# A fused four-layer decoder on one core: the masked attention's bias half on VectorE, the row maxima's split on GpSimd, and a new step table

## What is computed

```python
scores = jnp.einsum('bhqd,bhkd->bhqk', Q, K) / jnp.sqrt(jnp.float32(D))
scores = scores + adj[None, None, :, :]
scores = jnp.where(mask == 0, jnp.float32(-jnp.inf), scores)
weights = jax.nn.softmax(scores, axis=-1)
out = jnp.einsum('bhqk,bhkd->bhqd', weights, V)
```

## Time and profile before

| | us |
|---|---|
| median of 3 runs | 1161.64 (1161.58 to 1163.73) |
| the profiled execution | 1165.91 |
| its span | 1164.2 |
| PE busy / DVE busy / ACT busy / POOL busy | 1086.9 / 907.9 / 690.8 / 330.2 |

### The profile page before, as it was taken

One profiled execution on the slowest core, in us unless ns is written; L12 is line 12 of the kernel. 1 busy time (PEld: TensorE's weight loads), 2 busy tenths in 40 slices (PEclk: granted clock), 3 DMA queues, 4 the chain that ended last, 5 costly groups with the idle time before them and its releaser, 6 DMA issues. The chain is left out here.

```text
span 1164.2 us, 24274 instructions
## 1 busy us (share of the span) xinstructions
PE 1086.9 (93%) x8050; PEld 691.2 (59%) x8059; DVE 907.9 (78%) x2316; ACT 690.8 (59%) x1488; POOL 330.2 (28%) x443
## 2 busy tenths in 40 slices
PE   6877989999999998999999999999899999999998
PEld 2223554567777775677544444665667676775576
DVE  6999788977898898666679972417899999987754
ACT  4544687865545559775656544446566566558562
POOL 4546222112121111012213323211474445421010
PEclk9989698999999999999989999999999999999999
DMA  8003243222312331134423433141010001114211
GB/s 251 1 0 101 79 145 124 67 74 92 93 58 82 104 107 56 39 101 124 133 83 105 165 147 119 33 134 32 15 51 1 1 19 42 60 34 155 66 42 60
DMA packets 75785, 93.00 MB, mean 80 GB/s; under 512 B 6536, under 2 KB 60272, under 8 KB 73840
## 3 DMA queue, kind: packets, MB, share of 16 engines
q1 hardware_dynamic: 74640, 89.34, 24.5%
q0 software_dynamic: 1024, 2.10, 0.6%
HBM read 64.25 MB, written 28.67 MB: 80 GB/s over the span
## 5 line engine op out<-in xcount | busy, mean ns | idle before, releaser
L1449 ACT ACTIVATE P<-bank 128x512 f32<-128x512 f32 (+1 forms) x448 | 228.5, 585 | 68.3 <-PE bank L1142 67.3
L1864 DVE TENSOR_REDUCE mx<-bank 128x2 f32<-128x512 f32 x320 | 200.2, 684 | 23.7 <-PE bank L1113 20.9
L1662 POOL TENSOR_SCALAR rstd<-mv 128x2 f32<-128x2 f32 x56 | 14.0, 250 | 452.1 <-DVE mv L1714 376.5
L1157 PE MATMUL bank<-P,V 128*32 128x256 f32 (+1 forms) x1536 | 101.7, 383 | 1.1 <-ACT P L1449 0.8
L1256 PE MATMUL bank<-xT,room 128*128 128x256 f32 x384 | 95.4, 386 | 0.0
L1262 PE MATMUL bank<-room 128*128 128x256 f32 x384 | 94.8, 385 | 0.0
L1113 PE MATMUL bank<-QKR 48*128 48x256 bf16 (+1 forms) x896 | 82.1, 278 | 8.9 <-ACT P L1449 3.9
L1142 PE MATMUL bank<-QKR 50*128 50x256 bf16 (+1 forms) x896 | 84.5, 277 | 3.4 <-ACT P L1449 1.3
L1672 POOL TENSOR_TENSOR qk<-qk,parts 128x256 f32<-128x256 f32 x56 | 38.3, 705 | 145.9 <-ACT parts L1418 145.9
L1256 PEld LDWEIGHTS bank<-xT,room 128*128 128x128 f32 x384 | 69.6, 190 | 16.5 <-issue 7.9
L1262 PEld LDWEIGHTS bank<-room 128*128 128x128 f32 x384 | 69.8, 190 | 14.7 <-issue 6.8
(11 more groups left out here) (288 smaller groups left out, 2381.2 us busy)
## 6 DMA issues: line engine op xcount, KB each, us to landing
QKR<-split_rows SPq DMA_DIRECT2D x112, 192.0 KB
room<-gate_rows SPq DMA_DIRECT2D x48, 256.0 KB, 3.7
split_rows<-parts SPq DMA_DIRECT2D x56, 192.0 KB, 2.3
split_rows<-parts SPq DMA_DIRECT2D x56, 128.0 KB, 2.0
room<-in_w SPq DMA_DIRECT2D x6, 1024.0 KB
room<-in_w SPq DMA_DIRECT2D x3, 2048.0 KB
split_rows<-parts SPq DMA_DIRECT2D x56, 64.0 KB, 1.7
room<-in_mask SPq DMA_DIRECT2D x4, 512.0 KB, 6.0
```

The source lines that it names most:

```text
L1157: last = nc.tensor.matmul(bk[32 * j:32 * j + 32, q0:S], V[:, n % 2, t, 8 * half + 4 * r + j, :], P[:, (e - 1 + j) % NBUF_P, t * S:t * S + ...
L1449: nc.scalar.activation(P[:, (e - 1) % NBUF_P, 0:width], psum(st, p)[:, 0:width], ACT.Exp, scale=SCALE).then_inc(read[k], 1)
L1864: V_.reduce_max(to, sc[:, :].rearrange("p (t s) -> p t s", t=TPB), AX.X).then_inc(read[k], 1)
```

## The change

1. `BY_PE` is 1: PE adds the bias through identity products to the first head of a pair only. For the second one DVE adds `biasf[:, 1]` to the scores in PSUM, writes the sum to `P`, and ACT exponentiates it there in place. The bank is given free by ACT's instruction, as before.
2. MS is done by POOL: a cast of `mx` to bfloat16 and a subtraction, positive, where DVE had negated; the rows of ones in `QKR` become -1.0. DVE waits, before the first maxima of a unit, until the splits of two units earlier are done.
3. Semaphores: `first_max` counts maxima for POOL, `biased` DVE's additions; `select_in` and `dz_exp` are folded into others.
4. `ORDER` is another string, for changed costs of these steps (P2 of MASKED 1.65 to 0.96 on PE plus 0.7 on DVE, MS 0.6 on POOL, STAT 1.1 instead of 0.95 on POOL). 2392 steps, FILL 130 matmuls instead of 129.

```diff
-BY_PE = 2
+BY_PE = 1
-    "BIAS": ((DVE, 1.15),), "SM": ((PE, 0.28), (DVE, 1.2)), "MS": ((DVE, 0.36),), ...
+    "BIAS": ((DVE, 1.15),), "SM": ((PE, 0.28), (DVE, 1.2)), "MS": ((POOL, 0.6),), ...
     if st[0] == "P2" and st[1] == MASKED:
-        return ((PE, 1.65), (ACT, 1.0))
+        return ((PE, 0.96), (DVE, 0.7), (ACT, 1.0))
 ORDER = (
-    "aaaaaaaababaccbebddacebaecbdaecdacbeddacebaebcdaceddbbaecacebbddaecaceddbabecacdedbbaecbdaecdacedbaceedbacebacdedbbaaecc"
+    "aaaaaaaababaccbebdacebddaecbaecdacebdabcebdaecbdacebdacedaceddbacedbabecbacebdaecbdacebdaecbddaeceaceddbabaeccdebndonabc"
...
@@ scalar engine, P2
+                        if st[1] == MASKED and p >= BY_PE:
+                            act.wait_ge(biased, NPAIR * st[2] + st[3] + 1)
+                            nc.scalar.activation(P[:, (e - 1) % NBUF_P, :], P[:, (e - 1) % NBUF_P, :], ACT.Exp, scale=SCALE).then_inc(read[k], 1)
+                            continue
@@ gpsimd
-            nc.gpsimd.memset(QKR[:, :, 1], 1.0).then_inc(consts, 1)
+            nc.gpsimd.memset(QKR[:, :, 1], -1.0).then_inc(consts, 1)
+                elif k == "MS":
+                    _, a, b, h = st
+                    n = unit[(a, b)]
+                    finished(pool, ("SM", a, b, HALF * h + HALF - 1))
+                    if a in (CAUSAL, MASKED):
+                        pool.wait_ge(first_max, causal_before(("SM", a, b, HALF * h + HALF - 1), 1))
+                    if n >= 2:
+                        full(pool, ("MT", units[n - 2][1], units[n - 2][2], h))
...
+                    link(nc.gpsimd.tensor_copy(hi, top_of))
+                    nc.gpsimd.tensor_tensor(low, top_of, hi, ALU.subtract).then_inc(shift_done, 1)
@@ vector, SM
+                    if i == 0 and unit[(a, b)] >= 2:
+                        dve.wait_ge(shift_done, 2 * unit[(a, b)] - 2)
@@ vector
-                elif k == "MS":
...
-                    link(V_.tensor_scalar(hi, top_of, -1.0, None, ALU.mult))
-                    V_.scalar_tensor_tensor(out=low, in0=top_of, scalar=-1.0, in1=hi, op0=ALU.mult, op1=ALU.subtract).then_inc(shift_done, 1)
+                elif k == "P2" and st[1] == MASKED:
+                    e = head_no(st, 1)
+                    if e > NBUF_P:
+                        full(dve, weighs(e - 1 - NBUF_P))
+                    dve.wait_ge(filled[k], e)
+                    V_.tensor_tensor(P[:, (e - 1) % NBUF_P, :], psum(st, 1)[:, :], biasf[:, 1, :], ALU.add).then_inc(biased, 1)
@@ vector, BIAS
+                        dve.wait_ge(biased, NPAIR * b)
```

More of the change, by code:

```diff
@@ L61 @@
     "MY": ((DVE, 0.9), (PE, 0.4)),
-    "STAT": ((DVE, 1.2), (POOL, 0.95)), "XB": ((POOL, 0.8),), "STAT2": ((DVE, 1.95), (POOL, 0.95)), "NORM": ((DVE, 0.62),), "XT": ((PE, 0.22), (ACT, 0.33)),
+    "STAT": ((DVE, 1.2), (POOL, 1.1)), "XB": ((POOL, 0.8),), "STAT2": ((DVE, 1.95), (POOL, 1.1)), "NORM": ((DVE, 0.62),), "XT": ((PE, 0.22), (ACT, 0.33)),
     "GQ": ((PE, 0.43), (ACT, 0.3)), "GS": ((PE, 0.43), (DVE, 1.7)), "GT": ((PE, 0.44), (ACT, 0.5)), "GM": ((PE, 0.86), (ACT, 0.3)),
@@ L65 @@
     "V": ((PE, 0.44), (DVE, 0.42)), "Z": ((PE, 0.86), (ACT, 0.48)),
-    "BIAS": ((DVE, 1.15),), "SM": ((PE, 0.28), (DVE, 1.2)), "MS": ((DVE, 0.36),), "MT": ((PE, 0.2), (ACT, 0.3)), "SHIFT": ((SP, 1.4),),
+    "BIAS": ((DVE, 1.15),), "SM": ((PE, 0.28), (DVE, 1.2)), "MS": ((POOL, 0.6),), "MT": ((PE, 0.2), (ACT, 0.3)), "SHIFT": ((SP, 1.4),),
     "P2": ((PE, 0.27), (ACT, 0.95)), "PA": ((PE, 0.95),), "PV": ((PE, 0.95), (ACT, 0.33)), "ZV": ((PE, 0.95), (DVE, 0.86)),
@@ L99, in cost @@
     if st[0] == "P2" and st[1] == MASKED:
-        return ((PE, 1.65), (ACT, 1.0))
+        return ((PE, 0.96), (DVE, 0.7), (ACT, 1.0))
     if st[0] == "STAT":
-        return ((DVE, 2.7 if SUBLAYERS[st[1]] == ("moe", DISPATCHED) else 1.55 if st[1] in RMS_SUBLAYERS else 1.2), (POOL, 0.95))
+        return ((DVE, 2.7 if SUBLAYERS[st[1]] == ("moe", DISPATCHED) else 1.55 if st[1] in RMS_SUBLAYERS else 1.2), (POOL, 1.1))
     if st[0] == "SM" and st[1] == MASKED:
@@ L481 @@
[L481 to L484, removed]
@@ L835, in full, with causal_before @@
             eng.wait_ge(filled[st[0]], banks_of(st) * count[st])
+        split_maxima = [st for st in steps if st[0] == "SM" and st[1] in (CAUSAL, MASKED)]
+        def causal_before(st, p):
+            return 2 * split_maxima.index(st) + p + 1
         def head_no(st, p):
@@ L983, in _ @@
                     full(sp, ("DO", 1, NBLOCK - 1))
-                    load(select, "select", select_in)
-                    load(one_of, "one_of", select_in)
+                    load(select, "select", lin_loaded)
+                    load(one_of, "one_of", lin_loaded)
                 elif st[:2] == ("LD", "ctx"):
```

66 lines of the change are left out of this document (31 added, 35 removed).

## The result

The change makes the kernel slower. In twelve runs each, the changed kernel takes 1169.91 us in the median (1165.80 to 1175.19) and the kernel before 1163.14 (1159.96 to 1169.47): ratio 1.0058, 95% interval 1.0038 to 1.0077. Measured once more later, beside other kernels, it was 1167.62 against 1162.97, ratio 1.0050 (1.0025 to 1.0075). The forecast was 1158, faster.

A forecast was written before the change was run, and what follows sets the result against it. PE was taken as the bound, with DVE only 9.7 us behind in the masked stage's first part. Terms -2.2 (masked stage) and -1.5 (early stages) gave -3.7 us: 1161.6 to 1157.9, said as 1158; range 1149 to 1169.

The forecast's parts named there:

- The start of the masked stage: Part 4's first step: moved steps make MASKED's first maxima start 3.3 us earlier, at 605.2 instead of 608.5.
- the early relief: From 120 to 600 us, DVE sheds most of 40 splits; PE idles less, gaining 1.5 us (0 to 5).
- DVE's work up to the last maxima: Masked stage: DVE's work rises from 73.2 to 90.4 us, a stretch of 97.4 us with its idle time.
- the last maxima themselves: Masked stage: last maxima done at 702.6 us, against 691.3 before; the early relief not yet taken off.
- The splits off the path: Part 3: splits on POOL come 0.1 to 0.6 us later plus a hop, covered by other PE work, costed at nothing.
- the rival by DVE's queue: Masked stage: additions waiting for P2 hold up maxima; over 11 us of DVE idle, 1166 us; chance 0.22.
- PE's tail in part 4: Masked stage, last score product to last P2: 8.1 us of P2 steps plus 9.9 other work, ending 2.2 us earlier.
- slower, by POOL's queue: Rival: SPLITs queue behind splits of maxima, late rows stall PE; one stall and clock fall 5.2 us, time 1165; chance 0.11.
- a few us of DVE at most and hardly on the path: Part 3: POOL's 28 us of new work holding up DVE instructions through shared SBUF interfaces.
- The sign of being wrong that was met: PE waiting for the rows' DMA more often than three times.
- part 5: Outside the masked stage: 1.5 us gained from 120 to 600 us; after MASKED's last P2, PE work unchanged within 1 us.
- part 4's reasoning: Masked stage to its last P2: DVE becomes the bound, so 22.6 us less PE work buys only 2.2 us.

The follow-up runs named there:

- t4_msonly: Kernel before, old step table, with only the splits of the maxima moved from DVE to POOL: 1166.74 us, ratio 1.0008 to the kernel before.
- r_after: The changed kernel itself, run and profiled a second time: 1167.62 us in the median, ratio 1.0050 to the kernel before.
- t12_allfills: The change with its last 621 steps in the old order and idle products ahead of masked-stage waits and other lulls: 1155.37 us, ratio 0.9945 to the kernel before.
- t1_newtable: Kernel before with only the new step table and costs, products still on PE and splits on DVE: 1197.40 us, ratio 1.0266.
- t5_dummy3: The change with three identity products per masked P2 put back on PE, their result overwritten: 1184.45 us, ratio 1.0160 to the changed kernel.
- t9_morefills: The change with idle products ahead of masked-stage waits and 37 more at its other lulls, new tail kept: 1166.63 us, ratio 1.0025 to the kernel before.

## Why the prediction was wrong

**What held.** The start of the masked stage: first maxima at 602.5 where 603.7 had been forecast with the early relief (605.2 less 1.5). How much of it the moved steps did was not tried by itself: the kernel before had falls at 460 and 588 us, of 3.4 us each, that the change doesn't have, and the change has others. Up to there the kernel before was granted 1.6 us less of the full clock than the change. DVE's work up to the last maxima, 91.3 against 90.4, and the last maxima themselves, 701.6 against 701.1. The additions, 0.692 against 0.688 us, and DVE above 90% there (92%), PE below 85% (83%); the stretch of 99.0 us lies between the 95 and 100 that had been named. POOL's 31.5 us more against 28. The splits off the path (t4_msonly). DVE did not idle for 11 us; it was 7.7, so the rival by DVE's queue is not what happened.

**The step that failed first is PE's tail in part 4,** the term of 18.0 us in "697.8 + 18.0 = 715.8". PE's last score product ended at 696.2, as forecast with the early relief (697.8 less 1.5). From there to the end of the last P2 it took 22.9 us, not 18.0, and 23.1 in r_after: from 692 to 708 us the clock was between 0.50 and 0.76. In t12_allfills, at the full clock, it took 20.2, with nine idle products in it. In r_after the stretch ahead of the tail was shorter by as much as the tail was long, so its last P2 came when it had been forecast; that is luck. I had put such a fall under "slower, by POOL's queue", once, for 5.2 us, with a chance of 0.11. It came four times in the stage, and three times in r_after. I had written down the two facts that make it likely, a dozen us of new idle time in PE and the window with 2.07 of 4 us busy ahead of a fall, and treated them as a rival and not as a term. At 3.3 us each, four falls are 13.2 us; 15.4 us of clock were measured, of which about 7 are time on the path by the estimate above. The price of one fall was itself low: the two windows of the earlier trace rows lose 3.3 us, but the next one, 180 to 184 us, stood at 0.55, so that this fall cost 5.1 us of clock. The Trainium skill, "TensorE: Matmul & The Clock Gate", section "HAM oscillation — how this bites in real kernels", describes a PE that is throttled again at each wait which its loop repeats. The trace agrees in part: four lulls, four falls in this execution, but the first of these lulls brought none in the kernel before nor in r_after.

**The mechanism I gave for that rival was wrong.** It was not the splits in POOL's queue: with them alone the ratio is 1.0008, and in the stage the SPLITs waited for ACT and not behind them. Two of the four lulls are DVE's normalization, stretched to 1.96 and 1.84 us beside POOL's BP; one is ACT's copy behind exponentials, of which some wait for additions; and one is the last batch's rows, late by 4.5 us. So the additions have a direct part in one lull of four, and the new order in two: it puts BP beside the second normalization and the 2 MB load behind the rows. The forecast knew that POOL's work can hold up instructions of DVE, and had put it at "a few us of DVE at most and hardly on the path"; here PE waited for it. The sign of being wrong that was met, more than three waits for the rows, also seems to come with the order: PE waits for them 3 times in the kernel before, 5 in t4_msonly, 6 in t1_newtable, whose splits are on DVE, and 7 in the change. None of these causes was taken away by itself; the fills took away the lulls.

**The second step that failed is in part 5**: "After the last P2 of MASKED, PE has the same work as before within 1 us." The work is the same, but not its order. From the first LA product on, the new table idles PE for 5 us more, and the stretch to the end is 3.9 us longer (7.3 in r_after, with two falls of the clock in it). In r_after this alone is more than the whole loss. I had looked at the order only around MASKED; a table found anew is new everywhere.

**A third point lies in part 4's reasoning.** "So DVE is now the bound" gave the right length of the stretch, but DVE alone does not bound it: with PE's products back it was 11.9 us longer at the same DVE work. Removing 22.6 us of products was worth 12 to 14.5 us, and all the rest of the change, its new order, its waits and the falls among it, cost 4.7 to 6.8 more than that. What each of these costs by itself is open, since they were only taken away together.

## What to carry to other kernels

Before you take work from a PE that is nearly always busy, ask where it will now wait and put the fall of the clock behind each of these waits into the sum as a term. If the lulls can't be avoided, put idle products directly ahead of the waiting one, where they run instead of the wait: here 42 of them were worth 0.8% to a kernel that was otherwise untouched, while the 96 of t5_dummy3, put where PE did not wait, cost some 12 to 14.5 us. It is no sure gain: the 37 more of t9_morefills bought nothing with the new tail, and in t12_allfills, with the old one, 4 to 6 us. And where a table is searched anew, compare it stretch by stretch up to the end: a cut at which both orders have listed the same steps lets you take each part from the better one.

## What the runs showed of the hardware that I had not expected

In the earlier trace rows a stretch with PE busy for 2.61 of 4 us passed without a fall. In the change another with 2.61 of 4, at 648 us, brought one (clock 0.71 and 0.86), and so did one whose longest wait was 1.65 us, at 620. In r_after the same wait, 1.64 us long, left PE busy for only 1.66 of 4 us, at 620, and brought none: the clock stayed at 1.00 through the next 4 us. The busy share of a stretch in the profile therefore didn't tell me whether its clock would fall. Runs of one program differ with it: beside r_after the kernel before took between 1154.69 and 1169.95 us, with clocks of 0.986 and 0.968. The falls that a profile shows are those of one execution. And a fall can outlast its cause: from 696 to 708 us PE was busy for 11.6 of 12 us, and its clock stayed between 0.50 and 0.53.

The pair of instructions of a normalization took 0.60 us at 644.0 before, with POOL idle. In the two profiles, before and after, 17 pairs took from 1.15 to 2.64 us, and in every one of them POOL was at work for 1 us or more. By these rows work on POOL can lengthen a step of DVE that PE waits for, though DVE isn't given any more to do.
